# Cross-attention and quantised FFN in one kernel: K and V halves by groups of tokens, fewer setup instructions, K in other memory, a new opening order

## The reference

```python
q = layernorm(x) @ Wq;  k = ctx @ Wk;  v = ctx @ Wv          # no affine part in the norm
x = x + softmax(q k^T / 8) v @ Wo + bo                       # per head
y = layernorm(x)                                             # then three bit-linear layers
g = silu(bitlinear(y, w_gate)); u = bitlinear(y, w_up)       # 2048 wide
x = x + bitlinear(g * u, w_down)
# bitlinear(a, w): a is rounded to 127/max|a| of its row, w to -1, 0, 1 times mean|w|
```

## Time and profile before

| | us |
|---|---|
| runs | 1117.29, 1112.37, 1117.36; median 1117.29 |
| profiled execution, its own time | 1116.96 |
| its span, first to last instruction | 1115.0 |
| TensorE busy | 1080.1 (97%) |
| VectorE busy | 978.3 (88%) |
| ScalarE busy | 747.3 (67%) |
| POOL busy | 502.3 (45%) |

### The profile page before, as it was taken

The page is one execution under the profiler, slowest core; times in us unless marked ns, Lnnn a source line. Parts: engine busy times, 40 slices in busy tenths (PEclk is TensorE's granted clock), DMA queues, the critical chain, the costliest instruction groups (busy, mean ns, idle before and its releaser), DMA issues.

```text
span 1115.0 us, 17523 instructions
## 1 busy us (share of the span) xinstructions
PE 1080.1 (97%) x5505; PEld 497.6 (45%) x5567; DVE 978.3 (88%) x2097; ACT 747.3 (67%) x955; POOL 502.3 (45%) x641
## 2 busy tenths in 40 slices
PE   8878999999999999999999999999999999999998
PEld 6443444444344444444444444444444444444443
DVE  5989989788889988888999988888889899998995
ACT  3988757766665667777666667777666666666543
POOL 1066636566444445555544346555533444344110
PEclk9999999999999999999999999999999999999999
DMA  9999564554455545456545553454546544554334
GB/s 351 277 245 166 96 117 86 93 112 113 80 121 114 113 104 117 88 104 119 116 100 103 117 119 86 104 118 105 105 105 120 121 102 107 104 109 95 77 70 99
DMA packets 355963, 133.80 MB, mean 120 GB/s; under 512 B 332448, under 2 KB 332960, under 8 KB 355360
## 3 DMA queue, kind: packets, MB, share of 16 engines
q1 hardware_dynamic: 355872, 132.70, 54.9%
HBM read 34.08 MB, written 16.78 MB: 46 GB/s over the span
## 4 chain that ended last, share of the span: by engine, by line
PE 67%; issue 2%; DMA 1%; DVE 1%; POOL 0%; SPq 0%; ACT 0%; ACTq 0%; DVEq 0%; POOLq 0%
PE ps L1349 30%; PE ps L1368 15%; PE ps L1288 7%; PE ps L1289 7%; PE ps L1291 7%; DMA FF<-FF 1%; PE ps L1276 1%; PE ps L1281 1%; DVE hm L1044 0%; DMA pT<-AT 0%; DVE FF L1035 0%; SPq L575 0%; POOL AT L690 0%; ACT FF L830 0%; ACTq L41 0%
## 5 line engine op out<-in xcount | busy, mean ns | idle before, releaser
L1349 PE MATMUL ps<-wgT,FF 128*128 128x512 bf16 x1024 | 263.1, 379 | 2.4 <-DMA FF<-FF 2.1
L1349 PE MATMUL ps<-wW,FF 128*128 128x512 bf16 x1024 | 262.8, 379 | 1.1 <-DVE FF L1035 1.0
L1368 PE MATMUL ps<-wW,FF 128*128 128x512 bf16 x962 | 218.6, 379 | 9.0 <-DMA FF<-FF 4.3
L821 ACT ACTIVATE FF<-ps,sgu 128x512 f32<-128x512 f32 x256 | 173.7, 681 | 77.0 <-PE ps L1349 75.0
L1035 DVE TENSOR_TENSOR FF<-FF,ps 128x512 f32<-128x512 f32 x256 | 173.5, 681 | 43.2 <-PE ps L1349 23.3
L830 ACT ACTIVATE FF<-FF,c 128x1024 int16<-128x1024 f32 x128 | 141.2, 1141 | 79.2 <-DVE c L1048 76.4
L682 POOL TENSOR_TENSOR AT<-AT,rd 128x512 f32<-128x512 f32 x64 | 67.7, 1057 | 225.4 <-DVE rd L1080 222.3
L1368 PEld LDWEIGHTS ps<-wW,FF 128*128 128x128 bf16 x1024 | 99.4, 98 | 128.1 <-issue 9.9
L1349 PEld LDWEIGHTS ps<-wW,FF 128*128 128x128 bf16 x1024 | 99.7, 98 | 123.3 <-DVE FF L1035 4.1
L1349 PEld LDWEIGHTS ps<-wgT,FF 128*128 128x128 bf16 x1024 | 97.7, 98 | 125.6 <-issue 5.8
L670 POOL TENSOR_TENSOR xhl<-xn,xhl 128x512 f16<-128x512 f32 x64 | 74.8, 1168 | 79.4 <-ACT xhl L837 79.4
(11 more groups left out here) (146 smaller groups left out, 1771.7 us busy)
## 6 DMA issues: line engine op xcount, KB each, us to landing
xr<-in_x SPq DMA_DIRECT2D x64, 256.0 KB, 2.8
out<-xr SPq DMA_DIRECT2D x64, 256.0 KB, 2.3
FF<-in_L_ffn_w_gate SPq DMA_DIRECT2D x4, 1024.0 KB, 13.3
wW<-in_L_ffn_w_up SPq DMA_DIRECT2D x4, 1024.0 KB, 15.2
FF<-in_L_ffn_w_down SPq DMA_DIRECT2D x4, 1024.0 KB, 6.1
FF<-FF SPq DMA_TRANSPOSE x192, 3.3
MV<-in_L_xattn_Wq SPq DMA_DIRECT2D x1, 1024.0 KB, 5.5
MV<-in_L_xattn_Wo SPq DMA_DIRECT2D x1, 1024.0 KB, 13.3
```

The lines of the kernel that those rows point to most:

```text
L821: eng.activation(h[:, i % 2, f * 512:(f + 1) * 512], G[n % 2][:, :], ACT.Silu, scale=sgu[:, 0, i % W:i % W + 1]).then_inc(a_si, 1)
L1349: mm = eng.matmul(bank[n % 2][:, :].rearrange("p (o f) -> p o f", o=4), qxT[:, i % 2, k, :], w[:, 4 * f:4 * f + 4, k, :], start=(k == 0), ...
L1368: mm = eng.matmul(y_bank(i)[:, :], hT[:, i % 2, c, :], wdT[:, c, :], start=(c == 0), stop=(c == 15))
```

## The change

1. **Halves of K and V by tokens.** `c_hi m z` and `c_lo m z`: z = 0 takes tokens 0 to 127 (batches 0 and 1) of all four quarters, 512 elements per partition; z = 1 takes the other 384 tokens, 1536 elements. Each has a semaphore of its own. `round_X` waits for z = 0 alone, `pair_X` number 0 and 4 for z = 1.
2. **V's maximum** is one reduce over all 2048 elements (`max_v`). K's stays in four.
3. **Wo's halves** in two instructions of 1024 elements and not four of 512.
4. **scales** has one small instruction less: the power of two is put into an earlier one.
5. **K's quarters** lie in slots 7 to 10 of `xr`; `load_x` 7 to 10 wait for K's second low half.
6. **KEEP** and **OPENING** are written anew. A default time for the second job in one step goes from .24 to .3 (that job is named in both openings).

```diff
-        kT = MV[:, 0:2048].rearrange("p (q n) -> p q n", q=4)
+        kT = xr[:, 7:11, :]
-        KEEP = [('i', 22), ('i', 2), ('i', 9), ('t', 14), ('t', 4), ('t', 2), ('v', 1), ('v', 2), ('v', 3), ('v', 4), ('v', 44), ('v', 8), ('u', 14), ('u', 5), ('u', 24), ('v', 6)]
+        KEEP = [('i', 16), ('i', 1), ('i', 1), ('i', 9), ('i', 2), ('t', 3), ('t', 11), ('v', 27), ('v', 51), ('u', 2), ('u', 34)]
...
+                elif t >= 7:
+                    eng.wait_ge(v_cl[0][1], 1)
                 eng.dma_start(xr[:, r, :], x_t[t]).then_inc(l_x[r], 16)
...
+            def c_hi(m, z):
+                n = (slice(0, P), slice(P, D))[z]
                 eng.wait_ge(v_sk, m + 1)
+                eng.activation(split[m][:, :, 0, n], (kT, vT)[m][:, :, n], ACT.Copy,
+                               scale=kf[:, m:m + 1]).then_inc(a_ch[m][z], 1)
...
+            def max_v():
+                setup_done(eng, SETUP - 1)
+                eng.wait_ge(g_mc, 1)
+                eng.tensor_reduce(mxc[:, 3, 0:NB], vT.rearrange("p q (b l) -> p b q l", b=NB), AX_XY,
+                                  ALU.max, apply_absolute_value=True).then_inc(v_mx, 1)
...
-                link(eng.tensor_scalar(fwd[:, m, :], inv[:, m, :], we[:, m, 0:1], 2.0 ** -20, ALU.mult, ALU.mult))
-                eng.tensor_scalar(fwd[:, m, :], fwd[:, m, :], ke[:, m, 1:2], None, ALU.mult).then_inc(v_sc, 1)
+                eng.tensor_scalar(fwd[:, m, :], inv[:, m, :], we[:, m, 0:1], ke[:, m, 1:2], ALU.mult,
+                                  ALU.mult).then_inc(v_sc, 1)
...
+            def c_lo(m, z):
+                n = (slice(0, P), slice(P, D))[z]
+                eng.wait_ge(a_ch[m][z], 1)
+                eng.scalar_tensor_tensor(out=split[m][:, :, 1, n], in0=(kT, vT)[m][:, :, n], scalar=kf[:, m:m + 1],
+                                         in1=split[m][:, :, 0, n], op0=ALU.mult, op1=ALU.subtract
+                                         ).then_inc(v_cl[m][z], 1)
...
                 if r % 4 == 0:
-                    eng.wait_ge(v_cl, r + 4)
+                    eng.wait_ge(v_cl[r // 4][0], 1)
...
             def pair_X(b, r):
                 n = job(b, r)
+                if n in (0, 4):
+                    eng.wait_ge(v_cl[n // 4][1], 1)
```

More of the change, by code:

```diff
@@ L186, in xattn_ffn @@
         v_ol = sem("v_ol")
-        v_cl = sem("v_cl")
+        a_ch = [[sem(f"a_ch{m}{z}") for z in range(2)] for m in range(2)]
+        v_cl = [[sem(f"v_cl{m}{z}") for z in range(2)] for m in range(2)]
         a_hi = sem("a_hi")
@@ L292, in job_at @@
         def job_at(b, r, f):
[L293 removed]
+            return at(job_step(b, r), f + (.3 if r and job_step(b, r - 1) == job_step(b, r) else 0))
         SETUP = 15
@@ L380, in xattn_ffn @@
             "sync": (
-                "load_wq, load_ctx, load_wk, load_x 0, load_gate 0, load_gate 2, load_x 1, load_wv, load_gate 1, "
-                "load_gate 3, load_up 0, load_x 3, load_wo, load_up 1, load_up 2, load_bo, turn_x 0, load_up 3, "
[16 rows of a table removed]
-            "gpsimd": (
[18 rows of a table removed]
-            "scalar": (
[30 rows of a table removed]
-            "vector": (
[38 rows of a table removed]
-            "tensor": (
[3 rows of a table removed]
-                "keep 5, max_turn 2, total 1, keep 6, max_spread 2, keep 7, max_turn 3, keep 8, max_spread 3, keep "
[18 rows of a table removed]
+                "load_ctx, load_wk, load_wq, load_x 0, load_x 1, load_gate 0, load_gate 1, load_gate 2, load_gate "
+                "3, load_wv, load_up 0, load_wo, load_up 2, load_x 2, load_up 1, load_x 3, load_up 3, turn_x 0, "
[17 rows of a table added]
+            "gpsimd": (
[5 rows of a table added]
+                "p_lo 6, x_lo 9, b_lo 5, p_norm 7, d_scale 1, x_lo 10, p_lo 7, add_bo 7, b_lo 6, add_bo 8, p_norm "
[12 rows of a table added]
+            "scalar": (
[30 rows of a table added]
+            "vector": (
[39 rows of a table added]
+            "tensor": (
+                "keep 0, setup 0, setup 1, setup 2, keep 1, setup 3, setup 4, max_turn 0, setup 5, setup 6, setup "
[21 rows of a table added]
         }
@@ L860, in _ @@
             for m in range(2):
-                for q in range(4):
-                    put(MAX_T[m] + 1.3 + .3 * q, c_hi, m, q)
-            for c in range(4):
+                put(MAX_T[m] + 1.3, c_hi, m, 0)
+                put(MAX_T[m] + 1.6, c_hi, m, 1)
+            for c in range(2):
                 put(26 + c, o_hi, c)
@@ L986, in lo @@
                                              ).then_inc(v_lo, 1)
-            def c_lo(m, q):
-                eng.wait_ge(a_ch, 4 * m + q + 1)
-                eng.scalar_tensor_tensor(out=split[m][:, q, 1, :], in0=(kT, vT)[m][:, q, :], scalar=kf[:, m:m + 1],
-                                         in1=split[m][:, q, 0, :], op0=ALU.mult, op1=ALU.subtract).then_inc(v_cl, 1)
+            def c_lo(m, z):
[4 more added lines that the diff above has]
+                                         ).then_inc(v_cl[m][z], 1)
             def o_lo(c):
                 eng.wait_ge(a_oh, c + 1)
-                eng.scalar_tensor_tensor(out=wo[:, 1, c, :], in0=wo_sb[:, c, :], scalar=wf[:, 1:2],
-                                         in1=wo[:, 0, c, :], op0=ALU.mult, op1=ALU.subtract).then_inc(v_ol, 1)
+                eng.scalar_tensor_tensor(out=wo[:, 1, 2 * c:2 * c + 2, :], in0=wo_sb[:, 2 * c:2 * c + 2, :],
+                                         scalar=wf[:, 1:2], in1=wo[:, 0, 2 * c:2 * c + 2, :], op0=ALU.mult,
+                                         op1=ALU.subtract).then_inc(v_ol, 1)
             def abs_sum(m, c):
@@ L1116, in _ @@
                 put(MAXW_T[m], max_w, m)
-                for q in range(4):
-                    put(SET_E[(3, 11)[m] + q] + .7, max_c, m, q)
+                if m == 0:
+                    for q in range(4):
+                        put(SET_E[3 + q] + .7, max_c, q)
+                else:
+                    put(SET_E[14] + .7, max_v)
                 for e, w in ((2 * m, (MAXW_T[0] + 1, MAX_T[0] + 3)[m]), (2 * m + 1, MAX_T[m])):
@@ L1123, in _ @@
                 put(MAX_T[m] + 1.2, scale_c, m)
-                for q in range(4):
-                    put(MAX_T[m] + 1.5 + .3 * q, c_lo, m, q)
+                for z in range(2):
+                    put(MAX_T[m] + 1.5 + .3 * z, c_lo, m, z)
                 put(MAX_T[m] + 1.4, scales, m)
-            for c in range(4):
+            for c in range(2):
                 put(26.1 + c, o_lo, c)
```

37 lines of the change are left out of this document (17 added, 20 removed), and 247 rows, old and new, of the table OPENING.

## The result

| | before | changed |
|---|---|---|
| median of 4 runs each | 1117.14 us (1112.37 to 1117.36) | 1104.9 us (1103.97 to 1105.34) |
| ratio | 1 | 0.9899, 95% interval 0.9872 to 0.9927 |
| profiled execution, span | 1116.96, 1115.0 us | 1105.04, 1103.2 us |

The change makes the kernel 12.2 us faster, 1.1%. The nearest case was the first rival, "the whole of TensorE's lead lives", with 1106 to 1109.5 and a chance of 0.15, and it fell short too, by 1.1 us.

The account below looks back on a forecast made before the run. TensorE bounds the kernel, with the vector engines setting the pace before 100 us. VectorE's lead of 5.2 us less 0.3 gave 4.9 off the profiled 1116.96: 1112.1, or 1112.3 as median, range 1106.5 to 1119.5.

Parts of the forecast that it names:

- first rival: TensorE's whole lead of 7.7 us, perhaps with some of its idle time, reaches the end: 1106 to 1109.5, chance 0.15.
- What bounds the kernel: TensorE, busy for 97% of the span; before 100 us the vector engines set the pace; nothing changes past 350 us.
- Loads: At the start, Wq loaded behind ctx and Wk brings K's first product 3.1 us earlier; 0.7 shows at once.
- Fewer instructions: In the opening, fewer reduces, splits and links save VectorE 2.0 us; bounds for both vector engines 0 and 3.2.
- Halves by tokens, K out of the way: Before batch 0's first folded pieces: the first half is enough for round_X 0 0, and the later second half costs nothing.
- The order's walk: VectorE's list followed to mult 0 0 near 101 us: VectorE 5.2 us ahead, TensorE 7.7 ahead at gate_up 0 2.
- the cap: From gate_up 0 2 on, TensorE keeps only VectorE's 5.2 us less 0.3 for rounding: 4.9.
- The price of sharing: VectorE clips stretched beside POOL's work in the opening: four hit would take 2.8 of the 4.9 us.
- The second half of V's split: At about 73 us, one VectorE instruction of 1.8 us makes POOL wait 0 to 1.8; 1114.1 if all reached TensorE.
- The slower rival: Attention sets the pace ahead of gate_up 0 0, with scores 5 at 107: 8.7 us slower, 1126, chance 0.13.
- The clock: TensorE at half rate for part of 40 to 60 us, 3.6 us; behind 100 us it costs 1.8; widens the range only.
- three signs of being wrong: Scores 5 behind 94, TensorE idle over 10 us from 100 to 350, or K's product starting behind 9.5.

Follow-up runs that it names:

- wq_first: The changed kernel with Wq first in the load queue again: 1105.02 us.
- parts_old_order: The changed kernel's instructions in the order and with the fillers of the kernel before: 1115.82 us, ratio 0.9987.
- vector_late: The changed kernel with four spare VectorE reduces, 8.8 us in all, ahead of mult 4, 7, 10 and 13: 1110.69 us.

## Why the prediction was wrong, step by step

- **What bounds the kernel** held: TensorE's order of time up to gate_up 14 0 carries the gain, and nothing moved behind it but 0.4 us at the very end.
- **Loads.** "I take 3.1 us": K's first product was 1.8 earlier (9.12 for 10.94), since it waited for ctx's evacuation and not for Wk. K's factor came at 25.2, for 25.8, so the next step, that only some of it lives, held; and wq_first shows no more than 0.5 us for the load order.
- **Fewer instructions.** Prices held: 2.27 for V's maximum (2.3), 1.81 for 1536 elements (1.8), 1.28 for each of Wo's (1.25 by its sum), 0.28 for the fused link. Only V's second half took more, 2.05 for 1.8. In the old order they bought nothing that can be told from zero (parts_old_order).
- **Halves by tokens, K out of the way.** The walk gave no time of its own to them, since it counted them in the order's. That was right in kind: undone singly in the new order they cost 2.2, 1.8 and 0.5.
- **The order's walk** held to about 1 us at every landmark, and the lead of 7.7 at gate_up 0 2 was measured as 7.8, with two misses of some 0.9 us that cancel. At mult 0 0 VectorE was 5.7 us ahead where the walk had 5.2.
- **The step that failed**: "TensorE can't keep more than VectorE gives it, as gate_up n waits for mult n-2. I take VectorE's 5.2 less 0.3". TensorE kept all 7.8, 2.9 more than the 4.9 taken, and so were the other leads of the new order kept. The wait for a mult did grow, from 1.0 to 2.4 us, and vector_late shows that VectorE's time counts in part, so the mechanism exists; it was taken as a full cap and was none. VectorE still idled for 30 us of those 250, as it had for 28, so its list had room to slide. Its instructions that meet POOL's also took 8.5 us less over the span; how much of the kept lead its idle time carries and how much this isn't separated. The prediction had this very argument under its first rival and set against it that "the old order had that too and still left waits". Of the old order's waits only 1.0 us were for a mult; the largest, 2.8 us, were for turned probabilities, and 2.0 of these went.
- **What it left out**: the order of the 250 us behind gate_up 0 2. The text said that the time changes by what gate_up 15 0 moves by, but summed only to gate_up 0 2 and put the rest at nothing, because the work there is the same. The same work in another order was worth another 3.6 us (2.5 to 4.7 in the new-order kernels). That is why even the rival fell short: 7.8 alone would be 1109.2. Of the 7.0 us between the sum's 1112.1 and the profiled 1105.04, 2.9 are the cap, 3.6 this term and 0.4 the end. Either of the first two alone would have left the time inside the range.
- **The price of sharing** had the wrong sign. It reckoned with up to four stretched clips. The third weight's clips took 0.68 each, one clip of the second took 1.11, and behind 100 us there were fewer meetings than before, not more.
- **The second half of V's split** did hold POOL up, as feared. In the changed kernel, VectorE's c_lo 1 1 and POOL beside it:

```profile
71.30 2.05 DVE L1005 SCALAR_TENSOR_TENSOR vhl<-MV,kf,vhl 128x1536 f16<-128x1536 f32 x1
```

```profile
70.13 1.61 POOL L675 TENSOR_TENSOR xhl<-xn,xhl 128x512 f16<-128x512 f32 x1
71.71 1.72 POOL L659 TENSOR_SCALAR ve<-mv 128x1 f32<-128x1 f32 x1
```

  The small rstd link took 1.72 where it takes 0.22, and ended with the split: 1.5 us of waiting, most of the 1.8 of the upper bound. The x_lo ahead of it took 1.61 where 1.16 is usual, but it would have ended at 71.29, before the split began, so its 0.45 isn't the split's; the stretched clip of 1.11 ran beside its start. The pieces met were x_lo 3 and rstd 5's link, not x_lo 4 and p_norm 2. Little of it, if any, reached TensorE: gate_up 0 0 was 1 us ahead of the forecast. No run leaves the meeting out. The Trainium skill's rule in "SBUF — State Buffer", section "Who interferes with whom", that one engine waits out the other's whole instruction at the shared ports, is borne out by the split and the link; the time that the prediction worked out from it (1114.1, if all reached TensorE) is not.
- **The slower rival** didn't come: scores 5 stood at 88.8 where it had 107, and it would have decided only from 98.3 on. **The clock** fell nowhere in the changed kernel's eight runs; in the kernel before filler against the fall is worth about 2 us, where the prediction had 3.6 us at half rate, 1.8 us lost, and took nothing for it. The fall from 49 to 52 us went with the old order, and this was a gain that the forecast might have named.
- **The chances.** With a walk that had TensorE's lead at 7.7, 0.15 for that lead to live was too little, and the range should have reached below it, since the waits of 7.8 us were known to be there to be won. (0.15 and half of 0.50 are 0.40, not 0.39.) None of the three signs of being wrong that it named came: scores 5 at 88.8, 5.4 us of idle time, K's product at 9.12. They watched for a slower kernel only; the one sign that missed was K's product, outside its 7.5 to 8.5.
